# The inverse sums of a softmax are stored turned by the transfer itself, not by TensorE and ScalarE

## The chip, the cores and the metric

The kernel runs on one core of one Trainium2 chip. The metric is the device time of one execution in microseconds (us), as the median of several runs. TensorE multiplies matrices, VectorE and ScalarE work on elements, GpSimd helps them, and SyncE's queue (SPq in the profile) issues the transfers that the core's 16 DMA engines carry out.

## The reference

One transformer layer on 2 x 512 tokens of width 512: a layer norm, multi-head latent attention with 32 heads, a layer norm of its result, a residual sum, and then a gated feed-forward block with low-rank terms, again between layer norms and with a residual sum. The part that matters here is the attention:

```python
scores = jnp.einsum('bhqd,bhkd->bhqk', qf, kf) * scale
scores = jnp.where(causal, scores, jnp.finfo(scores.dtype).min)
probs = jax.nn.softmax(scores, axis=-1)
o = jnp.einsum('bhqk,bhkd->bhqd', probs, v)
```

The softmax divides each row of exponentials by its sum. The kernel does that late: it multiplies the exponentials by the values first and scales the result by the inverse sums.

## The kernel before

The kernel goes through the 32 heads in 16 pairs. In each pair it has 16 units, one for each of 2 batch entries (b), 2 heads (h) and 4 blocks of 128 queries (i). A unit is a chain over three engines: `scores` on TensorE (L1034 to L1036), mask and maximum on VectorE (L694), exponentials with their row sums on ScalarE (L427), a transpose of the exponentials on TensorE (`turn_p`, L1078), and a move of the turned block out of PSUM by ScalarE (`move_p`, L435). Each engine runs an order written out by hand in a function `body(p)` over `k` from 0 to 15, with scores two units ahead of the exponentials' transposes, and the engines meet through semaphores. Between the units stand the preparation of the next queries (`query`, `rotate_swapped`, `rotate_own`), the absorbed weights of the next pair, and the product of exponentials and values (`output`, L1090).

After 8 units, that is one batch entry of one pair, called m (0 to 31, 2 for each pair), the row sums of 2 heads x 4 blocks are ready as a tile of 128 partitions (queries) by 8 columns. The way of their inverses is what the change touches:

- VectorE takes the reciprocal (`invert`, L702) at k = 7 for the even m and at k = 15 for the odd m.
- TensorE transposes the 128 x 8 tile to 8 x 128 in a free quarter of PSUM bank 2 (`turn_r`, L1099), at the head of the next unit's transposes (k = 8, or k = 0 of the next pair).
- ScalarE moves it from PSUM to `r8` in SBUF (`move_r`, L445), before that unit's `move_p`.
- SyncE stores `r8` in a scratch tensor in DRAM as 8 rows of 512 bytes (`send_r`, L242), waits for the landing, and loads it back in two transfers, each of them one head's 512 values spread to 64 partitions (L245), into `rsb`.
- VectorE scales the output by `rsb` (`scale_o`, L707), at k = 13 for the even m and at k = 6 of the next pair for the odd m.

SyncE's queue runs in order: for each pair `send_r(2p-1)`, the load of the next query weights (`load_sq`), `send_r(2p)`, the load of the next value weights (`load_sv`), and the store of the product of value and output weights (`store_wvo`). After the last pair but one it goes over to loading those products back in eight transfers `wv_raw` of 512 KB (L293); the last two stores of inverses stand between them. The last of the eight waits for ten split weights, then for `send_r(31)`, and is issued behind it. The output projection begins behind the last pair: it takes the 16 loaded weights (`split_weights`, ScalarE L450 and VectorE L720), and `scale_o(31)` stands on VectorE ahead of the weights 12 to 15.

Of the kernel before, what the change touches and what calls it, by code (L numbers as in the profile page):

```python
# [23 lines left out]
ACT = mybir.ActivationFunctionType  # L24
AX = mybir.AxisListType

P = 128
# [3 lines left out]
QB = SEQ // P  # L31
DC = D // P
H, PAIRS = 32, 16
# [11 lines left out]
UNITS = 2 * QB  # L45
RING = (0, 1, 2, 0, 1, 2, 0, 1, 2, 0, 1, 2, 0, 1, 2, 1)
BACK = [next(d for d in range(1, 17) if RING[k - d] == RING[k]) for k in range(16)]
PU = BATCH * UNITS
# [30 lines left out]
def build(nc, x_d, wa_d, lnw_d, cst_d, kcs_d, sq_d, sv_d, w13_d, bs_d, a13_d, a2_d, w2_d, b2_d, out_d):  # L79
    rinv_d = nc.dram_tensor("rinv_scratch", [2, QB, P], F32, kind="Internal").ap()  # L80
# [6 lines left out]
    ident = keep.take("ident", [P, P])  # L87
# [25 lines left out]
    qswp = att.take("qswp", [P, 2, SEQ])  # L113
# [5 lines left out]
    pt = att.take("pt", [P, 2, 2, QB, SEQ])  # L119
    r8 = qswp[0:2 * QB, 0, 0:P]  # L120
    negmax = small[:, 0:8]
    rsum = small[:, 8:24]
    rinv = small[:, 24:32]
# [64 lines left out]
    bank = [nc.alloc_psum_tensor(f"bank{i}", [P, 512], F32) for i in range(8)]  # L188
# [13 lines left out]
    def sems(phase, words):  # L202
        return Semaphores((n, nc.alloc_semaphore(f"{phase}_{n}")) for n in words.split())
# [7 lines left out]
    a = sems("attention", """sq_in sv_in wq_made wq_hi_made wq_split rope_hi_made rope_lo_made rope_split q_made q_rotated pe_added qt_hi_made qt_split  # L211
        s_made s_masked exp_made p_turned p_moved o_made rinv_made r_made r_moved r_out r_in o_scaled
        wvo_made wvo_moved wvo_out""")
# [10 lines left out]
    with block:  # L224

        @block.sync
        def _(sp):
# [11 lines left out]
            def send_r(m):  # L239

                sp.wait_ge(a.r_moved, m + 1)
                sp.dma_start(rinv_d.rearrange("h i q -> (h i) q"), r8).then_inc(a.r_out, 16)  # L242
                sp.wait_ge(a.r_out, 16 * (m + 1))
                for h in range(2):
                    sp.dma_start(rsb[RKV * h:RKV * (h + 1), :].rearrange("p (o n) -> p o n", o=1),  # L245
                                 rinv_d[h:h + 1].rearrange("h i q -> h (i q)").unsqueeze(0).to_broadcast([RKV, 1, SEQ]))\
                      .then_inc(a.r_in, 16)
# [17 lines left out]
            load_sq(1)  # L265
            load_sq(2)
            send_r(0)
            load_sv(1)
            store_wvo(0)
# [126 lines left out]
        def _(act):  # L396
# [41 lines left out]

            def move_r(m, turned=None, first=False):
                act.wait_ge(a.r_made, m + 1)  # L440
                if turned is not None:
                    act.wait_ge(a.p_turned, turned)
                if not first:
                    act.wait_ge(a.o_scaled, m)
                nc.scalar.activation(r8, bank[2][0:2 * QB, 3 * P:], ACT.Copy).then_inc(a.r_moved, 1)  # L445

            def split_weights(q):
# [36 lines left out]
            def body(p, first=False, last=False):  # L484
                for k in range(PU):
                    if last and k == 6:
                        split_output(0, 0)
                    if last and k in (13, 14):
                        if k == 13:
                            act.wait_ge(a.o_made, 2 * PAIRS - 1)  # L490
                        split_weights(k - 7)
                    if k == 0 and not first:
                        move_r(2 * p - 1, PU * p + 1)
                    if k == UNITS:
                        move_r(2 * p, PU * p + UNITS + 1, first)
                    move_p(PU * p + k, k, 2 * p - 1 + k // UNITS if k % UNITS == 0 and not first else None)
# [7 lines left out]
                    if k in ((2, 4) if first else (1, 4)):  # L504
                        h = k // 4
                        query_hi(4 * p + 2 + h, 1, h, None if first else PU * (p - 1) + UNITS + QB * (h + 1))
                    if k in (9, 12) and not last:
                        h = k // 12
# [14 lines left out]
            for t in range(TB + 4):  # L523
# [33 lines left out]
                if t in (TB + 1, TB + 3):  # L557
                    h = (t - TB - 1) // 2
# [13 lines left out]
            split_output(0, 1)  # L572
            move_r(2 * PAIRS - 1)
            for q in range(10, PAIRS):
# [89 lines left out]
        def _(dve):  # L664
# [33 lines left out]
            def invert(m, b, first=False):  # L698
                dve.wait_ge(a.exp_made, UNITS * (m + 1))
                if not first:  # L700
                    dve.wait_ge(a.r_made, m)
                nc.vector.reciprocal(rinv, rsum[:, UNITS * b:UNITS * (b + 1)]).then_inc(a.rinv_made, 1)  # L702
# [84 lines left out]
            for t in range(TB + 4):  # L787
# [5 lines left out]
                if 0 <= t - 3 < TB:  # L793
                    u = t - 3
                    lat, q = bank[2 + u % 2], u % QB
# [235 lines left out]
        def _(pe):  # L1031
# [38 lines left out]

            def turn_p(U, k, first=False, r=None):
                pe.wait_ge(a.exp_made, U + 1)
                if not first:
                    pe.wait_ge(a.p_moved, U - 1)
                if r is not None:
                    turn_r(r)
                for j in range(k % QB + 1):
                    last = nc.tensor.transpose(bank[2 + k % 2][:, j * P:(j + 1) * P], pr[:, k % 4, j * P:(j + 1) * P],  # L1078
                                               ident[:, :])
                last.then_inc(a.p_turned, 1)  # L1080

            def output(m, b, js, first=False):
# [10 lines left out]
                if QB - 1 in js:  # L1093
                    last.then_inc(a.o_made, 1)

            def turn_r(m):

                pe.wait_ge(a.rinv_made, m + 1)
                nc.tensor.transpose(bank[2][0:2 * QB, 3 * P:], rinv, ident[:, :]).then_inc(a.r_made, 1)  # L1099

# [22 lines left out]
            def body(p, first=False, last=False):  # L1123
                for k in range(PU):
# [24 lines left out]
                    if k in (13, 15) and not last:  # L1149
                        query(4 * p + 6 + k // 15, 1, k // 15)  # L1150
                    turn_p(PU * p + k, k, first and k < 2,
                           2 * p if k == UNITS else 2 * p - 1 if k == 0 and not first else None)
                    if first and k < 2:
# [62 lines left out]

            turn_r(2 * PAIRS - 1)
            pe.wait_ge(a.s_masked, PU * PAIRS)
# [71 lines left out]
            for t in range(TB):  # L1290
                if t == 1:
                    lora_down(1, RT - 1)
                hf, q = t // QB, t % QB * P
# [88 lines left out]
```

## Time and profile before

| | |
|---|---|
| median of 3 runs | 595.21 us (594.8 to 596.28) |
| the profiled execution's own time | 596.79 us |
| its span, first to last instruction | 594.8 us, at a mean granted TensorE clock of 0.991 |
| busy | TensorE 562.7 us, VectorE 447.6, ScalarE 399.8, GpSimd 214.2 |
| transposes of the inverse sums | 32, of 273 ns each by the profile |
| moves of the turned sums by ScalarE | 32, of 252 ns each |

The profiled execution is 1.58 us above the median, and 1.99 us of its own time lie outside the span. Busy times are shares of the whole; which engine sets the pace is read stage by stage. Matmuls overlap in the pipeline, so the duration of one is more than the time after which the next starts.

### The profile page before, as it was taken

What the parts mean: (1) busy time and instruction counts of PE and PEld (TensorE: products, weight loads), DVE (VectorE), ACT (ScalarE), POOL (GpSimd) and SP (SyncE); (2) the same over time, 40 slices, a digit from 0 to 9 for tenths busy, and PEclk for the clock granted to TensorE, in tenths of its full rate; (3) what the DMA queues carried; (4) which work ended last, traced back from release to release, by engine and by line L of the source; (5) the groups of instructions that cost most, each with busy time, mean ns of one, the idle gap of its engine ahead of it and who ended that gap; (6) DMA issues with size and microseconds to landing.
All of it is one profiled execution on the core that took longest, in us unless ns stands there. A gap on an engine that the chain in (4) does not pass through costs nothing. (4 is left out here: it accounts for less than half of the span.)

```text
span 594.8 us, 10807 instructions
## 1 busy us (share of the span) xinstructions
PE 562.7 (95%) x3336; PEld 432.8 (73%) x3336; DVE 447.6 (75%) x1203; ACT 399.8 (67%) x1157; POOL 214.2 (36%) x204
## 2 busy tenths in 40 slices
PE   4789999999999999999999999999889999979996
PEld 4677778777787787787787877876568888745564
DVE  4886787787777777777877877778668889878466
ACT  4456778787887787787878877877653455355444
POOL 2234354444444543544444445432000000036520
PEclk9998999999999999999999999999999999999998
DMA  8101223213312322222123123025490000101003
GB/s 333 35 1 32 76 70 106 77 51 94 108 49 77 108 68 77 71 103 77 51 94 108 49 81 108 33 78 175 168 357 10 1 1 1 31 1 53 1 18 125
DMA packets 19560, 46.92 MB, mean 79 GB/s; under 512 B 2608, under 2 KB 3120, under 8 KB 19248
## 3 DMA queue, kind: packets, MB, share of 16 engines
q1 hardware_dynamic: 19504, 46.23, 23.4%
q8 instruction: 28, 0.46, 0.3%
q14 instruction: 28, 0.23, 0.1%
HBM read 39.80 MB, written 6.42 MB: 78 GB/s over the span
## 5 line engine op out<-in xcount | busy, mean ns | idle before, releaser
L694 DVE CUSTOM_DVE_ANT_0 ss<-bank,cst 128x128 f32<-128x128 f32 (+3 forms) x256 | 125.2, 490 | 85.0 <-PE bank L1036 64.1
L435 ACT ACTIVATE pt<-bank 128x128 f32<-128x128 f32 (+3 forms) x256 | 109.9, 429 | 65.5 <-PE bank L1078 65.2
L427 ACT ACTIVATE pr<-ss,small 128x128 f32<-128x128 f32 (+3 forms) x256 | 142.5, 557 | 6.3 <-DVE small L694 3.7
L329 POOL TENSOR_TENSOR qrot<-qrot,qswp 64x512 f32<-64x512 f32 x64 | 82.2, 1284 | 104.2 <-DVE qrot L686 101.7
L1078 PE MATMUL bank<-ident,pr 128*128 128x128 f32 x640 | 114.3, 276 | 1.0 <-ACT pr L427 0.9
L336 POOL TENSOR_TENSOR qt_lo<-qrot,qt_hi 128x512 fp32r<-128x512 f32 x64 | 82.1, 1283 | 69.8 <-ACT qt_hi L417 68.6
L1034 PE MATMUL bank<-kt_hi,qt_hi 128*128 128x128 f32 (+3 forms) x256 | 100.3, 392 | 1.8 <-DVE small L694 1.3
L1078 PEld LDWEIGHTS bank<-ident,pr 128*128 128x128 f32 x640 | 77.0, 141 | 22.4 <-issue 5.3
L1036 PE MATMUL bank<-kt_hi,qt_lo 128*128 128x128 f32 (+3 forms) x256 | 83.0, 324 | 0.0
L1035 PE MATMUL bank<-kt_lo,qt_hi 128*128 128x128 f32 (+3 forms) x256 | 82.7, 323 | 0.0
L1090 PE MATMUL bank<-pt,kvn 128*64 128x256 f32 (+3 forms) x512 | 75.2, 436 | 0.7 <-ACT pt L435 0.7
L1090 PEld LDWEIGHTS bank<-pt,kvn 128*64 128x64 f32 x512 | 35.5, 137 | 45.4 <-issue 34.2
L1034 PE MATMUL bank<-wv,o_s 128*128 128x512 f32 x128 | 51.6, 403 | 3.4 <-DVE wv L720 3.1
L391 POOL TENSOR_TENSOR fs<-gu 128x512 f32<-128x512 f32 (+1 forms) x6 | 8.8, 1465 | 124.7 <-DVE gu L968 124.6
L1034 PEld LDWEIGHTS bank<-kt_hi,qt_hi 128*128 128x128 f32 x256 | 48.6, 190 | 4.0 <-DVE small L694 1.8
L1035 PE MATMUL bank<-wv,o_s 128*128 128x512 f32 x128 | 50.5, 395 | 0.0
L1036 PEld LDWEIGHTS bank<-kt_hi,qt_lo 128*128 128x128 f32 x256 | 48.6, 190 | 2.7
L1036 PE MATMUL bank<-wv,o_s 128*128 128x512 f32 x128 | 50.5, 395 | 0.0
L1035 PEld LDWEIGHTS bank<-kt_lo,qt_hi 128*128 128x128 f32 x256 | 49.2, 192 | 0.1
L427 ACT ACTIVATION_READ_ACCUMULATOR pr<-ss,small 128x1 f32 x256 | 49.3, 193 | 0.0
L680 DVE TENSOR_TENSOR qswp<-bank,cst 32x512 f32<-32x512 f32 x64 | 44.5, 696 | 2.0
L681 DVE TENSOR_TENSOR qswp<-bank,cst 32x512 f32<-32x512 f32 x64 | 44.2, 691 | 0.9
(163 smaller groups left out, 1068.7 us busy)
## 6 DMA issues: line engine op xcount, KB each, us to landing
sv<-sv SPq DMA_DIRECT2D x16, 576.0 KB, 4.4
rsb<-rinv_scratch SPq DMA_DIRECT2D x64, 128.0 KB, 2.9
sq<-sq SPq DMA_DIRECT2D x16, 448.0 KB, 3.4
wvo_scratch<-vs SPq DMA_DIRECT2D x16, 256.0 KB, 2.2
wv_raw<-wvo_scratch SPq DMA_DIRECT2D x8, 512.0 KB, 4.4
xa<-x SPq DMA_DIRECT2D x8, 256.0 KB, 5.4
x<-x SPq DMA_DIRECT2D x1, 2048.0 KB, 10.0
out<-yo SPq DMA_DIRECT2D x8, 256.0 KB, 2.0
```

What stands on the lines that cost most here:

```text
L329: nc.gpsimd.tensor_tensor(qrot[RKV:P, h, :], qrot[RKV:P, h, :], qswp[RKV:P, h, :], ALU.add)\
L336: nc.gpsimd.tensor_tensor(qt_lo[:, b, h, :], qrot[:, h, :], qt_hi[:, b, h, :].bitcast(F32), ALU.subtract)\
L427: nc.scalar.activation(pr[:, k % 4, 0:n], ss[:, RING[k], 0:n], ACT.Exp, bias=negmax[:, k % 8:k % 8 + 1], scale=-1.0, accum_out=rsum[:, k:k ...
L435: nc.scalar.activation(pt[:, b, h, 0:i + 1, i * P:(i + 1) * P], bank[2 + k % 2][:, 0:(i + 1) * P].rearrange("p (j q) -> p j q", q=P), ACT. ...
L680: nc.vector.tensor_tensor(qswp[64:96, h, :], G[96:128, :], sin1[96:128, :], ALU.mult)
L681: nc.vector.tensor_tensor(qswp[96:128, h, :], G[64:96, :], sin1[64:96, :], ALU.mult)
L694: nc.vector.tensor_tensor_reduce(out=ss[:, RING[k], 0:n], in0=bank[k % 2][:, 0:n], in1=mask[:, SEQ - n:SEQ], scale=-SCALE, scalar=3.4e38, ...
L1034: nc.tensor.matmul(out, w_hi, x_hi, start=start, stop=False)
L1035: nc.tensor.matmul(out, w_hi, x_lo, start=False, stop=False)
L1036: return nc.tensor.matmul(out, w_lo, x_hi, start=False, stop=stop)
L1078: last = nc.tensor.transpose(bank[2 + k % 2][:, j * P:(j + 1) * P], pr[:, k % 4, j * P:(j + 1) * P], ident[:, :])
L1090: last = nc.tensor.matmul(bank[4][RKV * h:RKV * (h + 1), j * P:SEQ], kvn[:, QB * b + j, 0:RKV], pt[:, b, h, j, j * P:SEQ], start=(j == 0), ...
```

## The change

The transpose (`turn_r`), its move (`move_r`), the tile `r8` and two semaphores go. The store now reads the reciprocals as VectorE wrote them, 128 partitions by 8 values, and writes them transposed into the same scratch tensor: 1024 values of 4 bytes, none of them beside the next one of its partition. The store waits for the reciprocal and for the scaling before it. The reciprocal no longer waits for the transpose of the one before, but for the landing of its store. The two loads back are as before.

```diff
-    r8 = qswp[0:2 * QB, 0, 0:P]
...
             def send_r(m):
 
-                sp.wait_ge(a.r_moved, m + 1)
-                sp.dma_start(rinv_d.rearrange("h i q -> (h i) q"), r8).then_inc(a.r_out, 16)
+                sp.wait_ge(a.rinv_made, m + 1)
+                if m:
+                    sp.wait_ge(a.o_scaled, m)
+                with nc.allow_non_contiguous_dma("128x8 values are stored turned"):
+                    sp.dma_start(rinv_d.rearrange("h i q -> q (h i)"), rinv).then_inc(a.r_out, 16)
                 sp.wait_ge(a.r_out, 16 * (m + 1))
...
-            def move_r(m, turned=None, first=False):
-                act.wait_ge(a.r_made, m + 1)
-                if turned is not None:
-                    act.wait_ge(a.p_turned, turned)
-                if not first:
-                    act.wait_ge(a.o_scaled, m)
-                nc.scalar.activation(r8, bank[2][0:2 * QB, 3 * P:], ACT.Copy).then_inc(a.r_moved, 1)
...
                 if not first:
-                    dve.wait_ge(a.r_made, m)
+                    dve.wait_ge(a.r_out, 16 * m)
                 nc.vector.reciprocal(rinv, rsum[:, UNITS * b:UNITS * (b + 1)]).then_inc(a.rinv_made, 1)
...
-            def turn_p(U, k, first=False, r=None):
+            def turn_p(U, k, first=False):
                 pe.wait_ge(a.exp_made, U + 1)
                 if not first:
                     pe.wait_ge(a.p_moved, U - 1)
-                if r is not None:
-                    turn_r(r)
...
-            def turn_r(m):
-
-                pe.wait_ge(a.rinv_made, m + 1)
-                nc.tensor.transpose(bank[2][0:2 * QB, 3 * P:], rinv, ident[:, :]).then_inc(a.r_made, 1)
```

The calls of `move_r` and `turn_r`, two in the loop over units and one behind it on each engine, go as well.

## Rows read from the trace of the kernel before

**Rows 1.** The page's first part: busy time and share of each engine.
```profile
PE 562.7 (95%) x3336; PEld 432.8 (73%) x3336; DVE 447.6 (75%) x1203; ACT 399.8 (67%) x1157; POOL 214.2 (36%) x204
```

**Rows 2.** Windows, attention: length, busy by engine, PE clock, DMA share, GB/s.
```profile
100.00:400.00 300.00, 300.00 (x1983) 235.16 (x1980) 227.31 (x647) 238.58 (x760) 144.16 (x129) 1.00 0.25 80
```

**Rows 3.** TensorE's waits, 60 to 424 us: in total, times, longest.
```profile
PE bank L1099 <- ACT pr L427: 0.5, 1, 0.5
```

**Rows 4.** The removed transpose's line: duration shortest, median, longest, starts.
```profile
L1099 PE MATMUL bank<-ident,small x32: 271/273/273, 60.7 to 425.0; 128*8 128x128 f32 x32
```

**Rows 5.** TensorE's timeline around one removed transpose: start, duration.
```profile
247.35 0.34 PE L1036 MATMUL bank<-kt_hi,qt_lo 128*128 128x384 f32 x1
247.53 0.27 PE L1099 MATMUL bank<-ident,small 128*8 128x128 f32 x1
247.64 0.27 PE L1078 MATMUL bank<-ident,pr 128*128 128x128 f32 x1
...
247.98 0.40 PE L1035 MATMUL bank<-kt_lo,qt_hi 128*128 128x512 f32 x1
```

**Rows 6.** TensorE's timeline where the same neighbours stand without that transpose.
```profile
253.74 0.34 PE L1036 MATMUL bank<-kt_hi,qt_lo 128*128 128x384 f32 x1
253.92 0.27 PE L1078 MATMUL bank<-ident,pr 128*128 128x128 f32 x1
...
254.26 0.40 PE L1035 MATMUL bank<-kt_lo,qt_hi 128*128 128x512 f32 x1
```

**Rows 7.** The removed move's line on ScalarE.
```profile
L445 ACT ACTIVATE qswp<-bank x32: 250/252/267, 61.4 to 425.4; 8x128 f32<-8x128 f32 x32
```

**Rows 8.** SyncE's waits: in total, times, longest.
```profile
SPq L245 <- DMA rinv_scratch<-qswp: 30.8, 32, 2.6
```

**Rows 9.** SyncE's timeline: one store and its two loads.
```profile
248.47 0.30 SPq L242 DMA_DIRECT2D rinv_scratch<-qswp  x1
249.70 1.30 SPq L245 DMA_DIRECT2D rsb<-rinv_scratch  x2
```

**Rows 10.** Windows (as Rows 2): packets of a 4 KB store, of a 256 KB store.
```profile
249.23:249.34 0.11, 0.11 (x2) 0.01 (x1) 0.11 (x1) 0.11 (x1) 0.11 (x1) 1.00 0.20 38
...
254.98:255.97 0.99, 0.99 (x6) 0.77 (x5) 0.71 (x3) 0.99 (x6) 0.00 (x0) 1.00 0.70 265
```

**Rows 11.** DMA queue: packets, MB, share of 16 engines' span.
```profile
q1 hardware_dynamic: 19504, 46.23, 23.4%
```

**Rows 12.** VectorE's timeline: reciprocal and scaling of one even and one odd m.
```profile
246.08 0.20 DVE L702 RECIPROCAL small<-small 128x8 f32<-128x8 f32 x1
...
255.88 0.69 DVE L707 TENSOR_TENSOR ot<-bank,rsb 128x512 f32<-128x512 f32 x1
...
257.88 0.20 DVE L702 RECIPROCAL small<-small 128x8 f32<-128x8 f32 x1
...
268.45 0.69 DVE L707 TENSOR_TENSOR ot<-bank,rsb 128x512 f32<-128x512 f32 x1
```

**Rows 13.** The chain that ended last, 419 to 438 us: start, duration.
```profile
425.35 0.28 ACT qswp L445
...
425.69 1.20 DMA rinv_scratch<-qswp
...
426.91 0.45 SPq L245
...
428.05 4.71 DMA wv_raw<-wvo_scratch
```

**Rows 14.** VectorE's timeline behind the last pair, idle before in brackets.
```profile
423.24 1.29 DVE L720 TENSOR_TENSOR wv<-wv_raw,wv 128x512 fp32r<-128x512 f32 x2 [1.26 <-ACT wv L450]
...
430.49 0.69 DVE L707 TENSOR_TENSOR ot<-bank,rsb 128x512 f32<-128x512 f32 x1 [3.02 <-DMA rsb<-rinv_scratch]
```

**Rows 15.** Windows (as Rows 2) of the last store: transfers ahead of it, none after.
```profile
424.60:425.80 1.20, 1.20 (x12) 0.87 (x9) 1.09 (x1) 0.52 (x3) 0.00 (x0) 1.00 0.41 154
425.80:426.40 0.60, 0.60 (x4) 0.47 (x4) 0.36 (x2) 0.60 (x2) 0.00 (x0) 1.00 0.00 0
```

More of the change, by code:

```diff
@@ L211, in build @@
     a = sems("attention", """sq_in sv_in wq_made wq_hi_made wq_split rope_hi_made rope_lo_made rope_split q_made q_rotated pe_added qt_hi_made qt_split
-        s_made s_masked exp_made p_turned p_moved o_made rinv_made r_made r_moved r_out r_in o_scaled
+        s_made s_masked exp_made p_turned p_moved o_made rinv_made r_out r_in o_scaled
         wvo_made wvo_moved wvo_out""")
@@ L491, in body @@
                         split_weights(k - 7)
[L492 to L495, printed above, removed]
                     move_p(PU * p + k, k, 2 * p - 1 + k // UNITS if k % UNITS == 0 and not first else None)
@@ L572, in _ @@
             split_output(0, 1)
-            move_r(2 * PAIRS - 1)
             for q in range(10, PAIRS):
@@ L1150, in body @@
                         query(4 * p + 6 + k // 15, 1, k // 15)
-                    turn_p(PU * p + k, k, first and k < 2,
-                           2 * p if k == UNITS else 2 * p - 1 if k == 0 and not first else None)
+                    turn_p(PU * p + k, k, first and k < 2)
                     if first and k < 2:
@@ L1215, in turn_y @@
                 nc.tensor.transpose(bank[4][:, 0:P], lt[:, u % 2, :, :].rearrange("p g n -> p (g n)"), ident[:, :]).then_inc(c.y_turned, 1)
-            turn_r(2 * PAIRS - 1)
             pe.wait_ge(a.s_masked, PU * PAIRS)
```

## The prediction

> **What bounds the kernel now.** I read the page's first part, then windows of the attention, then TensorE's own timeline, and last SyncE's and VectorE's timelines along the way of the inverse sums.
>
> The page gives TensorE 95% of the span [rows 1], but a share over the span says little, so the attention is read by itself. From 100 to 400 us TensorE is busy for 300.00 of 300.00 us, VectorE for 227, ScalarE for 239 [rows 2]. The profile models the ends of matmuls, so "busy" could hide a short wait. The starts tell: in [rows 5] and [rows 6] the same neighbours stand, once with the removed transpose between them and once without. From L1036 to the next L1035 it is 0.63 us with it (247.98 - 247.35) and 0.52 us without (254.26 - 253.74). So TensorE sets the pace, and one transpose takes 0.11 us of it, not the 273 ns of its record [rows 4], which overlap with its neighbours.
>
> Behind the last pair the picture changes: the chain that ended last runs through the last move of the turned sums, its store (1.20 us), the issue of the two loads, and the last load of projection weights, 4.71 us [rows 13]. There a slower store lies on the path.
>
> **What is removed.** There are 32 transposes. The one of m = 31 (425.0) lies behind the last pair, in the stretch treated below. Before one other TensorE had been idle for 0.5 us, waiting for an exponential [rows 3]; that time is not given back. The 30 others give 30 x 0.11 = 3.3 us. The 32 moves of 0.25 us [rows 7] free 8 us of ScalarE, which is idle for 61 of 300 us and for which TensorE does not wait in that stretch [rows 2]: I count nothing. If ScalarE were the pace, it would be up to 8 us; the zero waits of TensorE exclude it.
>
> **What the store costs.** Call X the time from the issue of a store to the issue of the first load behind it. Before, X is 1.22 us (248.47 to 249.70 [rows 9], 425.69 to 426.91 [rows 13]), of which SyncE waits 30.8 / 32 = 0.96 us [rows 8]. That store is 8 packets of 512 bytes. The new one is 1024 values of 4 bytes, by my reading a packet each, 64 for each of 16 engines if they split evenly. No row shows such a packet. From below: if tiny packets cost nothing, X stays 1.22. From above: the mean packet of the run took 0.234 x 16 x 594.8 / 19504 = 0.114 us [rows 11], at some 2.4 KB; 64 of them in a row would be 7.3 us and X 8.5 us.
>
> Between these far ends the nearest rows are the packets of two stores [rows 10]. The 8 of 512 bytes kept 16 engines 20% busy for 0.11 us: 0.20 x 16 x 0.11 / 8 = 0.044 us each, completion marks included. The 128 of 2 KB in the store of `vs`: 0.70 x 16 x 0.99 / 128 = 0.087 us each. The 1536 bytes between them cost 0.043 us, so 512 bytes cost 0.014 us, and 0.030 us remain for a packet with hardly any bytes. 64 of these are 1.9 us: X = 1.22 - 0.04 + 1.9 = 3.1 us. I take 3.1 and keep 1.22 and 8.5 as ends.
>
> The Trainium skill (VectorE: DVE Perf Modes, The three transpose paths) speaks against such a store: a plain copy that transposes by its access pattern is 19 times slower than the DMA's own transpose, given with 1309 ns for 128 x 128. Worked out as an estimate from that page, 19 x 1309 ns / 16 for a sixteenth of the values is 1.55 us, and X would be 2.7 us and the sum -2.5 us. No run here shows it.
>
> **Where the store is hidden.** The store no longer waits for TensorE and ScalarE, so it is issued right behind the reciprocal. The reciprocal of the even m ends at 246.28 and its scaling starts at 255.88; of the odd m, 258.08 and 268.45 [rows 12]. That is 9.60 and 10.37 us. The wake-up of SyncE takes 0.06 us (425.63 to 425.69 [rows 13]), and from the first load's issue to a scaling that waits for it 3.58 us pass (426.91 [rows 13] to 430.49 [rows 14]). So X may reach 9.60 - 0.06 - 3.58 = 5.96 us in the even m and 6.73 us in the odd ones before VectorE waits. At 3.1 us the loads are even issued earlier than before, at 246.34 + 3.1 = 249.4 against 249.70. If the cover is gone, the scaling stands first on VectorE's queue with the next unit's mask behind it, then ScalarE's exponentials, then TensorE.
>
> The new waits cost nothing: the scaling before stands ahead of the next reciprocal on VectorE (k = 6 against 7, 13 against 15), and it needed the loads that came behind the awaited store. SyncE's later issues of the pair (query weights, value weights, the store of `vs`) keep their order; at X = 3.1 none of them moves back.
>
> **The last store.** Of m = 31, SyncE has two conditions: ten split weights, ready at 423.24 + 1.29 = 424.53 [rows 14], and until now the move, ready at 425.63. The store is issued at 424.59 in place of 425.69, 1.10 us earlier. But the engines still carry a load of weights: they are 41% busy until 425.8 and idle behind it [rows 15], and the small packets may queue behind it. I take 0.7 of the 1.1 us. The loads, the last weights and `scale_o(31)` then move by X - 1.22 - 0.7, at 3.1 us by +1.2 us, all of it on the path [rows 13].
>
> **Sum.** -3.3 + 1.2 = -2.1 us. The profiled execution took 596.79 us, 1.58 above the median of 595.21, and would take 594.7; for the median 595.2 - 2.1 = 593.1 us. Less than 0.3%, 1.8 us, is about what a measurement of this kernel can't tell from no change. The forecast's own ends: with X at 1.22 and the whole 1.10 us won, -3.3 - 1.1 = -4.4 (590.8); -1.8 (593.4) is reached at X = 3.4.
>
> **The rivals.**
>
> *The gain is eaten by the last store.* With X between 3.4 and 6 us nothing waits in the loop, but the end moves by 1.5 to 4.1 us: -1.8 to +0.8 us, 593.4 to 596.0. For it speaks that 0.030 us for a packet is an extrapolation to 4 bytes; against it, that a packet would need 0.035 us or more (2.2 / 64), close to the 0.044 us of a packet of 512 bytes.
>
> *The slot is not given back.* TensorE's 0.11 us are filled by a wait for ScalarE or VectorE, because their chain is just as long. Then only the last store counts: +1.2, 596.4 us. Against it: 61 and 73 us of idle time on these engines in 300 [rows 2], and TensorE's starts that follow one another at the same distances with and without the transpose [rows 5, 6].
>
> *The store outlasts its cover.* The place is `scale_o` of every m, and it decides from X = 6.0 us on, that is 0.075 us for a packet. A mechanism would be that each 4-byte write has to read what lies around it first and the engines carry few of them at a time. At the upper end, X = 8.5 us, VectorE is late by 2.5 us in the even m and 1.8 us in the odd ones. The engines run ahead of each other by about a unit, (257.88 - 246.08) / 8 = 1.48 us [rows 12], and if that absorbs as much of each, 1.0 + 0.3 = 1.3 us are left for each of 15 pairs, 20 us, with 6.6 at the end and -3.3: about 618 us. Without the lead it is 4.3 x 15 + 3.3 = 68 us more than before, 663. For it: partial writes to DRAM are nowhere in the trace. Against it: 8.5 us is the price of packets of 2.4 KB. The Trainium skill (DMA: Bandwidth & Descriptors, Specifications) says that below 512 bytes the engine reads, modifies and writes, and (Rules for kernel authors) that a strided last dimension becomes one descriptor for each element and should be rearranged. By that rule this rival gains weight; no run here shows it yet.
>
> **Chances.** The forecast (X under 3.4) 0.58; the gain eaten 0.15; the slot not given back 0.07; the store outlasting its cover 0.20, since one unknown, X, decides and its upper end lies beyond the limit. So faster 0.58, within 0.3% 0.22, slower 0.20. The range goes from 590.8 to the dearest case that is not a stall, 596.4, with 0.6 us for the spread of single runs (594.8 to 596.28): 590.8 to 597.0, which leaves out the 0.20.
>
> **What would show it.** In the profile after, SyncE's wait for the store's landing, 0.96 us before, gives X: some 2.8 us right, over 5.7 us the stall. TensorE's L1036 to L1035 should be 0.52 us at k = 0 and 8, and a pair 0.22 us shorter. VectorE should wait for the loads only once, at m = 31, at some 1.2 us later against its neighbours than before. Waits of VectorE for the loads inside the pairs would make the prediction wrong, and so would a store that lands as fast as before, then by up to 2.3 us on the other side.

## The result, and the profile after

The changed kernel takes 764.81 us (median of 4 runs, 761.21 to 767.37), the kernel before 595.75 us beside it (4 runs, 594.8 to 598.41): a ratio of 1.2803, interval 1.2755 to 1.2852. The forecast was 593.1 us. The profiled execution took 761.21 us, its span is 759.4 us, against 596.79 and 594.8 before: 164.6 us more in the span.

The page after: busy time and share of each engine, the granted clock in 40 slices, the packets, the DMA queue, the chain that ended last by engine, the line of `scale_o` with its idle time, and the loads with their median time from issue to landing.

```profile
PE 626.3 (82%) x3304; PEld 461.1 (61%) x3304; DVE 448.5 (59%) x1203; ACT 399.5 (53%) x1125; POOL 213.4 (28%) x204
...
PEclk9999888988889897889889899897987799999998
...
DMA packets 52328, 46.92 MB, mean 62 GB/s; under 512 B 35632, under 2 KB 35888, under 8 KB 52016
...
q1 hardware_dynamic: 52272, 46.23, 21.3%
...
DMA 62%; PE 14%; DVE 12%; issue 6%; ACT 3%; SPq 2%; POOL 1%; POOLq 0%; DVEq 0%; ACTq 0%
...
L696 DVE TENSOR_TENSOR ot<-bank,rsb 128x512 f32<-128x512 f32 x32 | 22.1, 692 | 142.1 <-DMA rsb<-rinv_scratch 142.1
...
rsb<-rinv_scratch SPq DMA_DIRECT2D x64, 128.0 KB, 3.9
```

VectorE's work is the same as before (448.5 us, [rows 1]: 447.6). ScalarE has 32 records less and, since others became longer, the same sum (399.5 against 399.8). TensorE went from 95% of the span to 82%. The queue has 52272 - 19504 = 32768 more packets for the same 46.23 MB [rows 11]: 1024 for each of 32 stores, as the prediction read the change. What bounds the kernel now is not an engine's work. The chain that ended last is DMA for 62% of the span.

The waits, in total, times, longest, first of the engines, then of SyncE ([rows 3] and [rows 8] are the rows of before):

```profile
DVE ot L696 <- DMA rsb<-rinv_scratch: 142.1, 32, 10.1
ACT pr L429 <- DVE small L683: 123.5, 80, 6.1
...
PE bank L1023 <- DVE small L683: 86.5, 40, 5.0
...
SPq L247 <- DMA rinv_scratch<-small: 315.3, 31, 12.1
```

This is the order that the prediction's third rival names: VectorE waits in `scale_o` of every `m` (142.1 / 32 = 4.4 us each), ScalarE waits for VectorE's masks behind it, TensorE for the masks' bank. SyncE waits 315.3 / 31 = 10.2 us for a store to land, against 0.96 us [rows 8]. The prediction had named over 5.7 us as the sign of the stall.

SyncE's timeline, start and duration, where [rows 9] showed 248.47 and 249.70:

```profile
252.22 0.38 SPq L244 DMA_DIRECT2D rinv_scratch<-small  x1
261.63 1.09 SPq L247 DMA_DIRECT2D rsb<-rinv_scratch  x2
...
268.97 0.37 SPq L244 DMA_DIRECT2D rinv_scratch<-small  x1
280.27 1.09 SPq L247 DMA_DIRECT2D rsb<-rinv_scratch  x2
```

X, from the issue of a store to the issue of its loads, is 9.41 us here and 11.30 in the next `m`. Over all 32 it goes from 8.37 to 12.46, mean 10.52. One pair lasts from 252.22 to 285.09 (the chain below), 32.87 us, where before it was 23.32 (248.47 [rows 9], and 271.79 for the next even `m`).

The chain of waits of that pair, start and duration:

```profile
252.22 9.40 DMA rinv_scratch<-small
...
262.13 5.43 DMA rsb<-rinv_scratch
...
267.58 0.04 DVE ot L696
...
268.82 0.12 DVE small L691
...
268.97 11.29 DMA rinv_scratch<-small
...
280.76 3.13 DMA rsb<-rinv_scratch
...
283.92 0.04 DVE ot L696
...
285.09 9.19 DMA rinv_scratch<-small
```

The whole pair is one ring: store, loads, scaling, a mask or two, the next reciprocal, the next store. Of 32.87 us, 9.40 + 11.29 = 20.69 are the two landings and 5.43 + 3.13 = 8.56 the loads. No matmul stands on it.

**Where the 164.6 us are.** SyncE's timeline, the stores of `m` = 0 and `m` = 30 and the last loads:

```profile
57.59 0.39 SPq L244 DMA_DIRECT2D rinv_scratch<-small  x1
...
553.73 0.36 SPq L244 DMA_DIRECT2D rinv_scratch<-small  x1
...
587.55 1.09 SPq L247 DMA_DIRECT2D rsb<-rinv_scratch  x2
```

The same two stores in the kernel before (its last loads are issued at 426.91 [rows 13]):

```profile
61.65 0.35 SPq L242 DMA_DIRECT2D rinv_scratch<-qswp  x1
...
410.51 0.29 SPq L242 DMA_DIRECT2D rinv_scratch<-qswp  x1
```

From the store of `m` = 0 to that of `m` = 30 it is 553.73 - 57.59 = 496.14 us, before 410.51 - 61.65 = 348.86: +147.3 us for 15 pairs, 9.8 each. The way from there to the issue of the last loads, from 553.73 to 587.55, takes 33.8 us against 16.4 (410.51 to 426.91): +17.4. The first store is issued 4.1 us sooner. 147.3 + 17.4 - 4.1 = 160.6; from the issue of the last loads to the last scaling it is 1.9 us more, and 2.0 us come behind it.

**What the store does while SyncE waits.** Windows of the store issued at 252.22: length, busy time by engine, TensorE's clock, DMA share, GB/s ([rows 10] before):

```profile
253.11:253.82 0.71, 0.20 (x2) 0.00 (x0) 0.70 (x2) 0.00 (x0) 0.00 (x0) 0.84 0.66 6
253.90:261.60 7.70, 7.26 (x29) 3.46 (x30) 3.79 (x10) 2.52 (x7) 3.80 (x3) 0.58 0.03 2
```

All packets pass within 0.71 us, with the 16 engines 66% busy: 0.66 x 16 x 0.71 / 1040 = 0.007 us for a packet, completion marks counted in. Then the engines are all but idle (3%) for 7.7 us, until the landing is reported, and the 3% are no work of the store: they are one load of instructions of 16 KB, which took 4.15 us. So the packets are cheaper than the 0.030 us that I had extrapolated, and the store is dearer. What takes the time lies behind the engines' packets, and the experiments ask what it is.

### The profile page after: what moved, and what is told of

Same layout as the page of the kernel before. It is cut to its first block, busy times and chain, and to the rows that moved or that the text cites. A ratio compares the mean times of both kernels' runs of the same rounds, so it can differ in the third digit from the quotient of the medians.

```text
span 759.4 us, 10709 instructions
## 1 busy us (share of the span) xinstructions
PE 626.3 (82%) x3304; PEld 461.1 (61%) x3304; DVE 448.5 (59%) x1203; ACT 399.5 (53%) x1125; POOL 213.4 (28%) x204
## 3 DMA queue, kind: packets, MB, share of 16 engines
q1 hardware_dynamic: 52272, 46.23, 21.3%
## 4 chain that ended last, share of the span: by engine, by line
DMA 62%; PE 14%; DVE 12%; issue 6%; ACT 3%; SPq 2%; POOL 1%; POOLq 0%; DVEq 0%; ACTq 0%
DMA rinv_scratch<-small 43%; DMA rsb<-rinv_scratch 17%; PE bank L1023 4%; PE bank L1025 4%; PE bank L1024 4%; SPq L247 2%; DVE ss L683 2%; DVE dot L871 1%; DMA wv_raw<-wvo_scratch 1%; DMA wd<-w 1%; DMA xa<-x 1%; DVE st L845 1%; DVE small L691 1%; DVE o_s L715 1%; DVE st L764 0%
## 5 line engine op out<-in xcount | busy, mean ns | idle before, releaser
L1023 PE MATMUL bank<-kt_hi,qt_hi 128*128 128x128 f32 (+3 forms) x256 | 109.1, 426 | 87.9 <-DVE small L683 86.5
L1065 PE MATMUL bank<-ident,pr 128*128 128x128 f32 x640 | 119.4, 286 | 8.7 <-ACT pr L429 8.6
L696 DVE TENSOR_TENSOR ot<-bank,rsb 128x512 f32<-128x512 f32 x32 | 22.1, 692 | 142.1 <-DMA rsb<-rinv_scratch 142.1
L1077 PE MATMUL bank<-pt,kvn 128*64 128x256 f32 (+3 forms) x512 | 93.6, 515 | 0.7 <-ACT pt L437 0.7
L1024 PE MATMUL bank<-kt_lo,qt_hi 128*128 128x128 f32 (+3 forms) x256 | 90.0, 351 | 0.0
L1025 PE MATMUL bank<-kt_hi,qt_lo 128*128 128x128 f32 (+3 forms) x256 | 89.4, 349 | 0.0
L1077 PEld LDWEIGHTS bank<-pt,kvn 128*64 128x64 f32 x512 | 41.7, 163 | 66.5 <-issue 58.1
L1025 PEld LDWEIGHTS bank<-kt_hi,qt_lo 128*128 128x128 f32 x256 | 54.2, 212 | 3.6
L1024 PEld LDWEIGHTS bank<-kt_lo,qt_hi 128*128 128x128 f32 x256 | 54.3, 212 | 0.1
L669 DVE TENSOR_TENSOR qswp<-bank,cst 32x512 f32<-32x512 f32 x64 | 44.5, 695 | 2.0
```

The costliest lines, as they stand in the source:

```text
L669: nc.vector.tensor_tensor(qswp[64:96, h, :], G[96:128, :], sin1[96:128, :], ALU.mult)
L696: nc.vector.tensor_tensor(ot[:, b * QB:(b + 1) * QB, p, :], bank[4][:, :].rearrange("p (t n) -> p t n", t=QB), rsb[:, :].rearrange("p (t n ...
L1023: nc.tensor.matmul(out, w_hi, x_hi, start=start, stop=False)
L1024: nc.tensor.matmul(out, w_hi, x_lo, start=False, stop=False)
L1025: return nc.tensor.matmul(out, w_lo, x_hi, start=False, stop=stop)
L1077: last = nc.tensor.matmul(bank[4][RKV * h:RKV * (h + 1), j * P:SEQ], kvn[:, QB * b + j, 0:RKV], pt[:, b, h, j, j * P:SEQ], start=(j == 0), ...
```

## The experiments

Theories at the outset: **shared lines** (small writes that fall into the same few bytes of DRAM go one after another), **count** (each small write to DRAM costs, wherever it goes), and **packets** (the engines' handling of them).

**Shapes of stores, first set.** The kernel before, with one more store of constants in 13 of its steps, into a scratch of its own; SyncE waits for its landing and then issues a small marker, so that store to marker is X. (Shortened: `flat` is the scratch as one row of values; semaphores are left out.)

```diff
+ # a: 1024 values turned, 4 KB, as the change stores them
+ sp.dma_start(flat[0:8 * P].rearrange("(c q) -> q c", q=P), values)
...
+ # b: the same, each value 64 bytes from the next
+ sp.dma_start(flat[0:8 * P * 16].rearrange("(c q w) -> q c w", q=P, w=16)[:, :, 0:1], values...)
...
+ # c: not turned, 128 rows of 32 bytes
+ sp.dma_start(flat[0:8 * P].rearrange("(q c) -> q c", q=P), values)
...
+ # d: 512 values turned, 2 KB
+ sp.dma_start(flat[0:4 * P].rearrange("(c q) -> q c", q=P), values[:, 0:4])
```

> The kernel before with one more store in 13 of the 32 steps, of constants, into a scratch tensor of its own that nobody reads; SyncE waits for its landing, VectorE and TensorE do not. Four forms take turns: (a) 1024 values of 4 bytes turned into 4 KB, as in the change; (b) the same 1024 values, each 64 bytes from the next; (c) 128 rows of 32 bytes; (d) 512 values of 4 bytes turned into 2 KB. Time from issue to the next issue. Theory count (the memory takes each small write by itself, about 8 ns each wherever it goes): (a) 9 us, (b) 9 us, (c) 2.2 us, (d) 5.3 us. Rival shared lines (values of one 64-byte line, sent by different engines, get in each other's way): (a) 9 us, (b) 2 to 3 us, (c) 2 us, (d) 5.3 us. Rival packets (the 16 engines themselves need the time): (a) 9, (b) 9, (c) 2, (d) 5 us, but then the DMA share is high for all of it. The kernel's time: within 1% of before.

SyncE's timeline, one store of each of the four and its marker:

```profile
163.12 1.28 SPq L260 DMA_DIRECT2D shape_scratch<-ident  x1
172.24 0.24 SPq L262 DMA_DIRECT2D mark_scratch<-ident  x1
...
187.47 0.43 SPq L264 DMA_DIRECT2D shape_scratch<-ident  x1
190.30 0.24 SPq L266 DMA_DIRECT2D mark_scratch<-ident  x1
...
210.80 0.43 SPq L268 DMA_DIRECT2D shape_scratch<-ident  x1
212.61 0.24 SPq L270 DMA_DIRECT2D mark_scratch<-ident  x1
...
234.12 0.43 SPq L272 DMA_DIRECT2D shape_scratch<-ident  x1
242.44 0.23 SPq L274 DMA_DIRECT2D mark_scratch<-ident  x1
```

In all: a 9.12, 9.68, 9.83; b 3.40, 2.83, 2.89, 2.84; c 2.15, 1.81, 1.83; d 9.61, 8.32, 9.08 us. The same 1024 values of 4 bytes take a third of the time when they lie apart, and half as many take as long when they lie together. Count falls, and with it packets, since a and b send the same ones. The one run took 607.81 us, 1.6% over the 598.03 of the kernel before beside it and more than expected; VectorE waited for the loads in 6 places, 12.8 us in all, where before it did in one, 3.0 us.

**Second set.** The same frame, four other stores: e, 1024 values 8 bytes apart; f, 512 bytes apart; g, only 128 values side by side, 512 bytes in all; h, 1024 values into SBUF, there too 8 bytes apart. (Shortened as above. This set and the next two took 597.21, 597.87 and 599.92 us, one run each.)

```diff
+ # g
+ sp.dma_start(flat[0:P].rearrange("(q c) -> q c", q=P), values[:, 0:1])
...
+ # h
+ sp.dma_start(small[:, 32:48].rearrange("p (c w) -> p c w", w=2)[:, :, 0:1], values...)
```

> As the run with four forms of store, with four others: (e) 1024 values of 4 bytes, not turned, 8 bytes from each other, so that one partition's 8 values lie in one 64-byte line; (f) 1024 values, each 512 bytes from the next; (g) 128 values of 4 bytes side by side, one of each partition; (h) 1024 values of 4 bytes into SBUF, each partition into its own. Theory count: (e) 9 us, (f) 9 us, (g) 2.2 us, (h) some 2 us, as SBUF takes small writes at once. Rival shared lines: (e) 3 to 5 us, (f) 2 to 3 us, (g) 2.2 us, (h) 2 us. Rival packets: (e), (f) and (h) 9 us, (g) 2.2 us.

SyncE's timeline, one store of g and one of h, each with its marker:

```profile
114.21 0.43 SPq L268 DMA_DIRECT2D shape_scratch<-ident  x1
122.62 0.24 SPq L270 DMA_DIRECT2D mark_scratch<-ident  x1
...
138.61 0.69 SPq L272 DMA_DIRECT2D small<-ident  x1
140.98 0.24 SPq L274 DMA_DIRECT2D mark_scratch<-ident  x1
```

e 6.68, 6.75, 7.55; f 3.46, 2.80, 2.90, 2.91; g 8.41, 7.38, 7.72; h 2.37, 2.37, 3.65 us. I had expected 2.2 us of g, and this miss decides most: 128 small writes, an eighth of the change's, cost nearly as much as 1024, if as many fall into the same place. And 1024 writes into SBUF, spaced as in e, landed in 2.4 us (3.65 once), against 6.7 to 7.6 in DRAM, so it is the DRAM side.

**Third set: how wide the place is.** 128 values, one from each partition, 8, 16, 32 and 64 bytes apart.

```diff
+ sp.dma_start(flat[0:P * w].rearrange("(q w) -> q w", w=w)[:, 0:1], values[:, 0:1])   # w = 2, 4, 8, 16
```

> As the runs with forms of store, now each form writes 128 values of 4 bytes, one of each partition, 8, 16, 32 and 64 bytes from each other; side by side they took 7.4 to 8.4 us. Theory shared lines (the writes that fall into one line of memory are carried out one after another, some 0.45 us each behind 1.3 us): with lines of 64 bytes 8, 4, 2 and 1 writes to a line: 4.9, 3.1, 2.2 and 1.8 us; with lines of 128 bytes all of them move by one step: 8, 4.9, 3.1 and 2.2 us. Rival (a store pays once for having any shared line): all about 8 us down to the line's size, then 2 us.

Side by side (g) 7.4 to 8.4 us; 8 bytes apart 5.07, 4.29, 6.01; 16 bytes 2.50, 4.54, 2.74, 2.52; 32 bytes 2.43, 2.11, 1.81; 64 bytes 1.82, 2.12, 2.48. From 32 bytes on nothing more is gained. So the shared place is 32 or 64 bytes; these steps do not tell the two apart. The means are 7.84, 5.12, 3.08, 2.12 and 2.14 us, close to the steps expected. Counted in 64 bytes, from 16 writes to one, it is (7.84 - 2.14) / 15 = 0.38 us for each further write; counted in 32 bytes, from 8 to one, it is 0.81. For 1024 values (a, b), counted in 64 bytes, it is (9.54 - 2.99) / 15 = 0.44 us.

**Fourth set: who sends them.** i, 128 values side by side, 16 from one partition; j, 16-byte runs side by side; k, 8-byte runs side by side; l, 8-byte runs 16 bytes apart. The kernel and frame are the same.

> Four more forms. (i) 128 values of 4 bytes side by side, the 16 of a 64-byte line all from one partition; (j) 128 runs of 16 bytes side by side; (k) 128 runs of 8 bytes side by side; (l) 128 runs of 8 bytes, 16 bytes from each other. Theory (writes to one line go one after another, whoever sends them): (i) 8 us as from 16 partitions, (j) 3 us, 4 writes to 64 bytes, (k) 5 us, 8 writes, (l) 3 us, 4 writes. Rival (only different engines get in each other's way): (i) 2 us, the others as before, since each run comes from another partition. If the number of small writes counted and not their lines, (j), (k) and (l) would be alike.

i 7.14, 6.75, 10.00; j 2.90, 3.03, 2.83, 1.82; k 4.32, 3.63, 3.03; l 1.84, 2.11, 3.29 us. That one partition sends all writes of a place does not help (i against g). Longer runs do, as there are fewer writes to a place; k, with 8 writes to 64 bytes, stayed under the 5 us expected.

**The landing alone.** Nothing of the kernel before is taken out; before each store of the inverse sums SyncE stores constants turned, as the change does, and waits for them.

```diff
+ sp.wait_ge(a.rinv_made, m + 1)
...
+ sp.dma_start(sh_d.rearrange("h i q -> q (h i)"), ident[:, 0:8]).then_inc(sh_in, 16)
+ sp.wait_ge(sh_in, 16 * (m + 1))
  sp.wait_ge(a.r_moved, m + 1)
```

> The kernel before, with nothing removed: TensorE still turns the inverse sums, ScalarE still moves them. Ahead of each of their 32 stores SyncE issues, as soon as the reciprocal is there, a turned store of 1024 constants of 4 bytes into another scratch tensor and waits for its landing. Theory (the landing of the turned store is all of the loss): the stores of the sums are late by as much as in the change and by their own 1.2 us more, so the time is that of the change, 765 us, plus 32 x 1.2 for the second landing and 3 for the transposes kept: 800 to 810 us. Rival (the loss comes from what was removed or from the values' new place, for example the reciprocals' tile being read late): 600 to 700 us.

It took 754.37 us. The waits of SyncE for that store and of VectorE in `scale_o`:

```profile
SPq L248 <- DMA shape_scratch<-ident: 225.9, 29, 9.3
...
DVE ot L713 <- DMA rsb<-rinv_scratch: 143.8, 32, 10.6
```

VectorE waits 143.8 us in 32 places, as in the changed kernel (142.1), although the transpose and the move are still there. The wait for the landing is the loss, and the rest of the change has next to nothing to do with it. The expected size was missed by some 50 us, as I had put the second landing on top of a first one as long as in the changed kernel. Measured from issue to issue (the 225.9 us above leave out waits put down to others), this store took 9.39 us in the mean, 8.24 to 10.75, against 10.52; the store of the sums behind it took 1.75, and the loads up to the scaling 3.87 against 4.76. From the turned store to the scaling that is 15.0 us here and 15.3 in the changed kernel, which is why the waits are alike.

**The rest of the change without the turned store.** The values are stored straight, in 32-byte rows, so the loads bring the sums in another order.

```diff
- sp.dma_start(rinv_d.rearrange("h i q -> q (h i)"), rinv)
+ sp.dma_start(rinv_d.rearrange("h i q -> (h i q)").rearrange("(q c) -> q c", q=P), rinv)
```

> The change with one thing different: the store writes the reciprocals as 128 rows of 32 bytes, not turned, so that the loads bring the inverse sums in the wrong order; the work is otherwise the same. It tells what the removal is worth with a store that lands soon. Theory: the transposes' slots are given back, 30 x 0.11 = 3.3 us, and with X of 1.3 to 2.5 us the last store moves the end by -0.6 to +0.6 us: 591.5 to 593.5 us, ratio 0.993 to 0.997. Rival (the slot is not given back): 595 to 596 us, ratio 1.000.

596.12 us (10 runs) against 598.03: 0.9968, interval 0.9939 to 0.9998, as expected. It is the prediction's sum without its dear term, and gains about 1.9 us. In its trace a pair lasts 23.19 us ((394.96 - 209.46) / 8 from SyncE's stores) against 23.32: 0.13 us are given back, not 2 x 0.11 = 0.22. TensorE's starts show where the rest goes: each transpose that is gone gives 0.10 us back on the spot (the 0.63 us of [rows 5] are 0.53 here, from 245.13 to 245.66), but of that of an even `m` 0.06 are lost again within the next ten matmuls.

Its profiled execution took 598.91 us, longer than its median, and shows two places behind the attention where a lead is lost. Its timeline, start and duration, idle time before in brackets:

```profile
428.14 0.69 DVE L696 TENSOR_TENSOR ot<-bank,rsb 128x512 f32<-128x512 f32 x1 [3.49 <-DMA rsb<-rinv_scratch]
...
429.49 0.80 PE L1023 MATMUL bank<-wv,o_s 128*128 128x512 f32 x1 [3.08 <-DVE wv L709]
...
540.58 1.49 ACT L631 ACTIVATE wd_hi<-wd 128x1536 fp32r<-128x1536 f32 x1 [1.49 <-DMA wd<-w]
543.35 1.26 POOL L393 TENSOR_TENSOR fs<-gu 88x512 f32<-88x512 f32 x1 [4.48 <-DVE gu L957]
543.52 1.64 DVE L972 TENSOR_TENSOR xf_lo<-xft,xf_hi 128x512 fp32r<-128x512 f32 x1
545.22 0.79 PE L1023 MATMUL bank<-xf_hi,w_hi 128*128 128x512 f32 x1 [2.41 <-DVE xf_lo L972]
```

The same places in the kernel before ([rows 14] has its last scaling, at 430.49):

```profile
431.83 0.50 PE L1034 MATMUL bank<-wv,o_s 128*128 128x512 f32 x1 [2.32 <-DVE wv L720]
...
540.75 1.49 ACT L642 ACTIVATE wd_hi<-wd 128x1536 fp32r<-128x1536 f32 x1 [0.40 <-DMA wd<-w]
543.78 1.93 POOL L391 TENSOR_TENSOR fs<-gu 88x512 f32<-88x512 f32 x1 [3.61 <-DVE gu L968]
543.89 0.67 DVE L983 TENSOR_TENSOR xf_lo<-xft,xf_hi 128x512 fp32r<-128x512 f32 x1
544.62 0.50 PE L1034 MATMUL bank<-xf_hi,w_hi 128*128 128x512 f32 x1 [0.52 <-DVE xf_lo L983]
```

The windows of TensorE's clock (the last three columns are clock, DMA share, GB/s) are these in the straight kernel:

```profile
432.00:434.00 2.00, 2.00 (x6) 1.52 (x6) 1.55 (x3) 0.20 (x1) 0.00 (x0) 0.50 1.01 362
```

and in the kernel before:

```profile
432.00:434.00 2.00, 1.50 (x6) 0.88 (x6) 0.88 (x2) 1.16 (x3) 0.00 (x0) 1.00 0.59 152
```

*First place.* The last scaling is 2.35 us ahead (428.14 against 430.49). TensorE's idle time is 3.08 us instead of 2.32, and behind it the granted clock is 0.50, the level of 1.2 GHz, where it stayed at 1.00 (2.4 GHz) before. Of the lead 1.29 us are left at 522 us (the same reciprocal of VectorE at 522.21 and 523.50). This is no mark of the straight kernel: in all seven other traces in which the clock had been at 1.00 up to here, it fell to 0.50 at this place too, in the four sets of stores, which keep the transposes, after 2.38 to 2.52 us without work. The one profiled execution of the kernel before is the exception; what its other executions do here is not on record.

*Second place.* At 540 us ScalarE waits 1.49 us instead of 0.40 for the load of `wd`, which landed later after its issue (540.58 - 535.49 = 5.09 us to the split, against 540.75 - 536.79 = 3.96). So the split begins 0.17 us ahead, no longer 1.3. Then VectorE and GpSimd start beside one another; before, it was GpSimd's instruction that became long (1.93 us), here it is VectorE's `xf_lo` (1.64 against 0.67), and TensorE waits 2.41 us in place of 0.52. At 577 us the kernel is 1.9 us behind (577.55 against 575.68). The late `wd` has a likely cause in the traces: in all five kernels with the change, the changed one included, a load of instructions of 16 KB, 0.89 to 0.96 us long, falls into the load of `wd`, which takes 5.09 to 5.49 us up to the split; in none of the six that keep the transposes does one, and there it takes 3.96 to 4.15. No run moved that load away to try it. A long `xf_lo` (1.72 us) is also seen in two kernels with a prompt `wd`, the fourth set of stores and the landing alone, where TensorE then waits 1.56 and 1.57 us.

**Values 64 bytes apart in the changed kernel.** The scratch is 16 times as large and filled once at the start; the loads read its first 4 KB, so they do not bring the inverse sums, but move as many bytes.

```diff
+ far_d = nc.dram_tensor("rinv_far", [2, QB, P, 16], F32, kind="Internal").ap()
...
- sp.dma_start(rinv_d.rearrange("h i q -> q (h i)"), rinv)
+ sp.dma_start(far_d.rearrange("h i q w -> q (h i) w")[:, :, 0:1], rinv.rearrange("p (c o) -> p c o", o=1))
```

> The change with one size different: the same 1024 turned values of 4 bytes go to a scratch tensor in which each is 64 bytes from the next. The loads read the first 4 KB of it, so they do not bring the inverse sums; all else is as in the change, in number of writes, waits and order. Theory shared lines: X is some 2.9 us, under the cover of 5.96 us, and the loss is gone: pairs of 23.2 us, 592 to 600 us, ratio 0.993 to 1.005. Rival (the number of 4-byte writes, or the turning as such): X stays at 9 to 11 us, 750 to 770 us.

598.72 us (10 runs) against 597.76: 1.0013, interval 0.9988 to 1.0039, from 764.81 with the same 1024 packets side by side. Its waits of VectorE and of SyncE:

```profile
DVE ot L701 <- DMA rsb<-rinv_far: 4.2, 1, 4.2
...
SPq L251 <- DMA rinv_far<-small: 74.4, 32, 3.1
```

X is 2.4 to 3.4 us, mean 2.71, and VectorE waits once, at the end, as the prediction described for its forecast of 3.1. A pair lasts 23.19 us. The last scaling starts at 429.52, 1.0 us ahead of the kernel before; the two places of the straight kernel follow (a granted clock of 0.50 from 430 to 436 us, a wait of 1.75 us for `wd`), and no gain is left. The store is turned and has as many packets as in the change; only the spacing differs.

**8 bytes apart, to try the limit of the cover.** The edit is the same with 2 in place of 16.

> As the run with 64 bytes between the values, with 8 bytes between them, so that 8 writes fall into each 64 bytes in place of 16. Alone such a store took 6.7 to 7.6 us. Theory (what exceeds the cover of 5.96 and 6.73 us is lost in full in each half of a pair): 0.7 to 2.4 us for each of 15 pairs and some 5 us at the end, less 2 us for the slots given back: 608 to 640 us, ratio 1.02 to 1.07. Rival (a lead of one unit, 1.48 us, absorbs that much of each lateness, as the prediction took it): only the end counts, 595 to 601 us, ratio 1.00 to 1.01.

602.77 us (10 runs) against 597.76: 1.0073, interval 1.0051 to 1.0095. Turned with 4, 8 and 64 bytes from value to value, X is 10.52, 4.54 and 2.71 us in the mean. Up to `m` = 29 X was 3.96 to 5.10 us, less than the 7 us of e, so it stayed under the limit, and neither theory was tried as meant; the time comes nearest to the second theory's, but not for its reason. VectorE waited in 2 places, 0.24 and 5.94 us, both in the last pair or behind it, and a pair lasted 23.19 us. The first is the scaling of `m` = 29 and tries a limit after all, as the last pair covers less: from its reciprocal's end to its scaling the kernel before has 406.49 - 398.00 = 8.49 us, and here it would have been 402.53 - 393.75 - 0.24 = 8.54 without the wait. X was 4.42 and the loads took 4.34 up to the scaling, 8.76 us together, which is over that by about the wait. The last scaling starts at 429.70, 0.8 us ahead. What is lost comes later: ahead by 0.95 us still at 522.55 (against 523.50), behind by 2.8 at 578.50 (against 575.68), with 1.89 us of waiting for `wd` between. That is the profiled execution, 599.47 us, the shortest of the ten; the other 3.3 us to the median aren't seen in it.

**Another way to turn the values.** VectorE transposes the reciprocals in 32 x 32 blocks, and four stores write 8 rows of 128 bytes each.

```diff
+ nc.vector.transpose(r32[:, 1, :], r32[:, 0, :]).then_inc(a.r_made, 1)
...
- sp.dma_start(rinv_d.rearrange("h i q -> q (h i)"), rinv)
+ for g in range(4):
+     sp.dma_start(rinv_d.rearrange("h i q -> (h i) q")[:, 32 * g:32 * g + 32], r32[32 * g:32 * g + 2 * QB, 1, :])
```

> The change with another way to turn: VectorE transposes the tile of reciprocals in blocks of 32 x 32 (columns 8 to 31 are zeros), and SyncE stores it in four transfers of 8 rows of 128 bytes, so that no 64 bytes of memory are written twice; the output is that of the reference. Theory shared lines: X (issue of the first store to the issue of the first load) is 2 to 2.6 us, of which three more issues are 0.9; VectorE has 0.2 to 0.4 us more to do 32 times and idles enough; TensorE's slots are given back. The time is 0.2 to 0.6% below before, ratio 0.994 to 0.998. Rival (small rows in DRAM are slow as such): X of 5 us or more, ratio 1.00 to 1.05.

599.62 us (12 runs) against 597.2: 1.0048, interval 1.0028 to 1.0069; the expected gain did not come. The store is as cheap as hoped, 2.16 us from its issue at 244.40 to that of the loads at 246.56, but a pair still lasts 23.32 us: VectorE's transpose takes 0.21 us for each `m`, and the 0.13 us that the other kernels got back are not seen. The two places behind the attention show here too (0.50 from 432 to 434 us, 1.74 us for `wd`).

No kernel tried here beats the one before, but for the straight store's 0.3%, and that one brings the sums in another order.

## Why the prediction was wrong

**What bounds the kernel: right before, not after.** TensorE set the pace. After, the ring of store, loads and scaling does.

**What is removed: right in kind, too large.** I counted 30 x 0.11 = 3.3 us. Three kernels without the transpose (straight, 64 and 8 bytes apart) give 0.13 us in a pair, 15 x 0.13 = 2.0 us. On the spot it is 0.10 us for each, close to my 0.11; that the starts behind it would keep all of it was the error. The rival "the slot is not given back" is thus true for the other 40%. Of ScalarE's 8 us no gain beyond these 2.0 is seen, as said.

**What the store costs: the step that failed.** X was put at 3.1 us, with ends at 1.22 and 8.5. It measured 8.37 to 12.46, mean 10.52, and the smallest of 32 is just under my upper end. The count of packets was right (1024 for each store), and my price for one was four times too high. The error was to bound the landing by the time of the engines at all: 0.7 us of the 10.5 are packets. The rest is the time until writes of which 16 fall into the same 64 bytes are done, 0.4 us or so for each further one; with the same packets 64 bytes apart, X was 2.71. My upper end came from packets of 2.4 KB, which do not share such a place, and so it was no upper end.

The mechanism that I gave to the rival, that a 4-byte write has to read what lies around it first, would fit the stores that share a place, but no run shows the reading; "the engines carry few at a time" does not fit, as 1024 such writes 64 bytes apart land in 2.8 to 3.4 us. The Trainium skill (DMA: Bandwidth & Descriptors, Specifications) puts a read, modify and write below 512 bytes. The runs agree that the store below 512 bytes is the dearer one, but its size alone does not make it dear: 128 rows of 32 bytes side by side landed in 1.8 to 2.2 us, and the values 64 bytes apart no slower than those 512 bytes apart. The Trainium skill's rule on transposing copies (VectorE: DVE Perf Modes, The three transpose paths), from which I had estimated X at 2.7 us, speaks against the change rightly; the measured 10.5 is four times the estimate, while the store that is turned with 64 bytes between the values, at 2.71, stays at the estimate.

**Where the store is hidden: the limits hold as far as they were tried.** At X of 2.4 to 5.1 us no `scale_o` before the last pair waits, and a pair is 23.19 us at either end; at 8.4 and more every one waits. Between them no kernel stood, so the 5.96 and 6.73 themselves weren't tried; in the last pair the cover read from the kernel before held within 0.05 us (values 8 bytes apart).

**The rivals.** "The store outlasts its cover" is what happened, in the place and order that it named; I gave it 0.20. Its 618 us rested on a lead of 1.48 us that would absorb part of each wait. Nothing of the kind is seen: the scaling stands first on VectorE's queue and holds the next reciprocal, so every wait is on the ring. The version without a lead, with X at 10.5, gives (10.5 - 5.96) + (10.5 - 6.73) = 8.3 us for each pair, against 9.8 measured. The loads too land later after their issue, 3.9 us in the median against 2.9 before, for which the sum had no term.

**The last store: right within 0.7 us.** At the last reciprocal (421.23 before) the straight kernel, 64 bytes, 8 bytes and VectorE's turn were 3.10, 2.17, 3.27 and 1.61 us ahead, at the last scaling 2.35, 0.97, 0.79 and 1.40. So the last store cost them 0.75, 1.20, 2.48 and 0.21 us; with X of 2.62, 3.44, 5.12 and 2.20 the prediction's X - 1.22 - 0.7 gives 0.70, 1.52, 3.20 and 0.28. In the changed kernel, where X is 9.34 there, the last pair as a whole cost 17.4 us.

**What the sum lacked.** That 2 us won by `scale_o(31)` are 2 us won at the end was taken for granted. In the four kernels with a cheap store the lead at 522 us (0.04 to 1.48) was gone at 577, where they were 0.6 to 2.8 us behind, in a stage whose work the change doesn't touch. All of this is against one profiled execution of the kernel before. The forecast's -2.1 us would thus not have been safe at X = 3.1 either: the kernel with X = 2.71 measured 1.0013.

**What stays open.** Whether the memory or the DMA engine's write side does the writes of one place in turn, and whether the place is 32 or 64 bytes. Why 1024 values 8 bytes apart took 6.7 to 7.6 us when one partition sent the eight of a place (e), and 4.0 to 5.1, once 6.3, when eight partitions did (turned, 8 bytes apart). Why X in the changed kernel has two sizes, some 9.3 us (8.4 once) and 10.3 to 12.5, where the turned store of constants took 9.1 to 9.8 (8.2 to 10.8 in the landing alone). Why the loads behind such a store land later; the two go together, as by the chain the loads take 4.5 to 5.7 us behind the shorter stores and 2.9 to 3.8 behind most of the longer ones. It is not only the loads: 16 KB of instructions whose load begins 2.8 us or more behind the issue of such a store take 3.0 to 4.4 us, all others 0.9 to 1.4. With the constants' store into another scratch (the landing alone) they take 0.9 to 1.3, once 2.2, and no run tells whether it is the place in DRAM that matters. And whether the load of instructions is what makes `wd` late, which is where a part of the small gains went.

## What to carry to other kernels

Before turning values by the address pattern of a transfer, count how many separate writes fall into the same 32 to 64 bytes of DRAM, not how many packets or bytes there are: here it was 16 in 64, and a store of 4 KB took 10.5 us in place of 1.2. The DMA's busy share does not show this; only the wait for the landing does, so the price of an unseen store is not bounded by the packet times of others. And ask of each transfer how late it may land before the ring of buffers closes: under that limit 1024 packets cost the loop nothing, beyond it every microsecond was paid, twice in each pair.

## What the runs showed of the hardware

- Small writes into the same 32 or 64 bytes of DRAM hold the landing up, by about 0.4 us for each further one if counted in 64 bytes: 128 values of 4 bytes side by side 7.4 to 8.4 us, the same 64 bytes apart 1.8 to 2.5 us; 1024 of them turned 9.1 to 9.8, 64 bytes apart 2.8 to 3.4. One partition as the sender of all writes of a place does not help (6.8 to 10.0). Into SBUF the 1024 took 2.4 us (3.65 once).
- A packet of 4 bytes occupies a DMA engine for 0.007 us (1040 of them in 0.71 us, 16 engines 66% busy).
- Behind the turned store of the changed kernel loads of 16 KB of instructions took 3.0 to 4.4 us, where they took 0.9 to 1.4 otherwise.
- After 3.08 us without work TensorE ran at a granted clock of 0.50 for over 4 us, and at the same place in four other traces it fell to 0.50 after 2.38 to 2.52 us; in the kernel before, after 2.32 us there, it stayed at 1.00.
- Where VectorE's `xf_lo` and GpSimd's `fs` start within 0.2 us of each other, one of them becomes long: 1.93 us for GpSimd with 0.67 for VectorE, or 1.26 with 1.64. With the first TensorE waited 0.52 us, with the second, and a late `wd`, 2.41.
